# Attention stage: the two norms leave VectorE, a loop is written out, and SyncE's transfers change their order

## The reference, cut to what matters

```python
q = rope(x @ Wq.T); k = rope(x @ Wk.T); v = x @ Wv.T      # 16 maps of 8 dims for each sequence
attn1, attn2 = sdpa(q1, k1, v1), sdpa(q2, k2, v2)          # softmax(q.k * 8**-0.25) @ v
o = attn1 - lam * attn2                                    # 8 heads of 16 values
o = o * rsqrt(mean(o*o over a head) + 1e-8)                # head norm
out = (o * ln_w + ln_b) * (1 - LAMBDA_INIT) @ Wo.T
x = layernorm(x + out)
```

## Time and profile before

| | |
|---|---|
| median of 3 runs | 1077.75 us (1073.69 to 1080.13) |
| the profiled execution, its own time | 1077.57 us |
| its span, first to last instruction | 1075.8 us |
| busy in the span | PE 86%, DVE 86%, POOL 74%, ACT 67% |
| mean granted TensorE clock | 0.957 |
| attention, `scores(0, 0)` to the last residual | 629.0 to 941.6 us |

### The profile page before, as it was taken

One profiled execution on the slowest core, in us unless ns is written; L12 is line 12 of the kernel. 1 busy time (PEld: TensorE's weight loads), 2 busy tenths in 40 slices (PEclk: granted clock), 3 DMA queues, 4 the chain that ended last, 5 costly groups with the idle time before them and its releaser, 6 DMA issues. The chain is left out here.

```text
span 1075.8 us, 15499 instructions
## 1 busy us (share of the span) xinstructions
PE 925.1 (86%) x4482; PEld 481.8 (45%) x4482; DVE 921.2 (86%) x1446; ACT 725.4 (67%) x1536; POOL 791.9 (74%) x576
## 2 busy tenths in 40 slices
PE   7697989797989797777887679999999997799995
PEld 2233434243434342335555454555555543345454
DVE  4799999999999999999883667898999974589996
ACT  4776868686868686444654467777777768777872
POOL 2899999989898989866777644566676534877772
PEclk9899999999999999898998889999999999999997
DMA  4752525253535342005201223232323210000001
GB/s 150 313 237 78 232 83 206 110 198 117 199 117 199 117 198 118 1 1 106 40 1 48 70 75 105 75 99 83 104 74 105 76 46 2 1 1 13 18 20 30
DMA packets 35164, 103.97 MB, mean 97 GB/s; under 512 B 3659, under 2 KB 22475, under 8 KB 24395
## 3 DMA queue, kind: packets, MB, share of 16 engines
q1 hardware_dynamic: 35095, 103.16, 27.9%
HBM read 93.84 MB, written 8.91 MB: 96 GB/s over the span
## 5 line engine op out<-in xcount | busy, mean ns | idle before, releaser
L610 PE MATMUL bank<-m_hC,ident 128*128 128x512 f32 x512 | 256.5, 625 | 61.8 <-POOL m_hC L568 23.5
L558 POOL TENSOR_TENSOR m_dBu<-m_du,m_Bt 128x1024 f32<-128x1024 f32 x128 | 299.5, 2358 | 11.9 <-DMA m_Bt<-bcd 11.1
L333 DVE TENSOR_TENSOR_SCAN bank<-bank,m_dBu 128x512 f32<-128x512 f32 x184 | 222.1, 1218 | 16.4 <-ACT bank L461 12.6
L1406 DVE TENSOR_REDUCE a_nm<-bank 128x2 f32<-128x512 f32 x256 | 169.3, 684 | 45.5 <-PE bank L1637 43.1
L1576 ACT ACTIVATE late<-bank 128x512 f32<-128x512 f32 x256 | 150.4, 598 | 75.3 <-PE bank L1637 73.7
L610 PEld LDWEIGHTS bank<-m_hC,ident 128*128 128x128 f32 x512 | 93.8, 195 | 201.9 <-issue 112.7
L461 ACT ACTIVATE bank<-m_delta,early 128x510 f32<-128x510 f32 x256 | 170.0, 677 | 0.3
L342 DVE TENSOR_TENSOR m_hC<-bank,m_Ct 128x512 f32<-128x512 f32 x184 | 122.7, 667 | 0.0
L568 POOL TENSOR_TENSOR m_hC<-m_hS,m_Ct 128x512 f32<-128x512 f32 x72 | 94.8, 1316 | 25.9 <-DVE m_hS L333 25.8
L1637 PE MATMUL bank<-ks,qs 72*128 72x256 bf16 x512 | 100.1, 279 | 14.5 <-DMA ks<-parts 8.0
L458 ACT ACTIVATE bank<-m_zero 128x2 f32<-128x2 f32 x181 | 31.2, 172 | 113.7 <-DVE m_hC L342 113.3
(11 more groups left out here) (218 smaller groups left out, 1843.6 us busy)
## 6 DMA issues: line engine op xcount, KB each, us to landing
m_Bt<-bcd SPq DMA_DIRECT2D x32, 1024.0 KB, 5.6
m_Ct<-bcd SPq DMA_DIRECT2D x32, 1024.0 KB, 6.4
qs<-parts SPq DMA_DIRECT2D x16, 576.0 KB
ks<-parts SPq DMA_DIRECT2D x48, 192.0 KB
parts<-a_part SPq DMA_DIRECT2D x32, 192.0 KB, 2.2
out<-x_all SPq DMA_DIRECT2D x8, 256.0 KB, 2.3
vx<-in_vrow SPq DMA_DIRECT2D x4, 256.0 KB
qs<-in_fill SPq DMA_DIRECT2D x1, 768.0 KB
```

Source lines behind the costliest of these rows:

```text
L333: nc.vector.tensor_tensor_scan(out, decay, dBu[:, g % RD], 0.0, ALU.mult, ALU.add).then_inc(scan_ready, 1)
L558: nc.gpsimd.tensor_tensor(dBu[:, g % RD:g % RD + CH], du[:, n % 2], Bt[:, s].unsqueeze(1).broadcast_to([P, CH, GTOK]), ALU.mult).then_inc( ...
L610: return nc.tensor.matmul(out, lhsT, rhs, start=start, stop=stop)
L1406: nc.vector.tensor_reduce(nm[:, slot % 2, q, 2 * pair:2 * pair + 2], s1[i % 2][:], AX.X, ALU.max, negate=True).then_inc(max_ready, 1)
```

## The change

The step is rearranged in five ways.

1. **Layer norm.** The output weights are centred once (`wo_c`: the mean of each row is subtracted), so that the projection's result has mean zero over the features; the layer norm then needs only the mean of squares. ACT computes it with two Square instructions that also sum (`squares`), POOL adds the epsilon, takes the power and multiplies once. DVE keeps the addition of the residual.
2. **Head norm.** The product with the reciprocal root goes from DVE (u = 5 of the next step) to POOL (directly behind the power, at u = 14).
3. **Places.** The difference and its followers go to earlier slots; queries and keys of group n + 4 are projected at u = 4 and u = 6 and exchange their banks; POOL's `rotate` waits for the difference; ACT's copy of part 0 goes from u = 0 to u = 15 of the step before; POOL's first subtraction goes ahead of the layer norm.
4. **SyncE.** The transfers of the maxima are issued behind the read back of queries and keys instead of ahead of the wait for the parts.
5. **Loop.** Steps 3 to 10 are written out.

```diff
     def sync(sp):
         def body(n, slot):
@@
             if has(n, 3):
                 sp.wait_ge(split_p, 2 * m + 2)
                 for i in range(2):
                     sp.dma_start(k.parts[i].rearrange("a p t -> p a t"), part[:, :, i, :]).then_inc(parts_out, 16)
-            if has(n, 1):
-                sp.wait_ge(nmT_ready, n + 2)
-                for a in range(3):
-                    sp.dma_start(qs[MROW + a:MROW + a + 1, (slot + 1) % RING],
-                                 nmT[MAPS * a:MAPS * a + MAPS, :]).then_inc(nm_in, 16)
             if has(n, 3):
                 sp.wait_ge(parts_out, 32 * m + 32)
...
                 for a in range(3):
                     sp.dma_start(ks[24 * a:24 * a + 24, s].rearrange("r m t -> r (m t)"), k3).then_inc(q_in, 16)
+            if has(n, 1):
+                sp.wait_ge(nmT_ready, n + 2)
+                for a in range(3):
+                    sp.dma_start(qs[MROW + a:MROW + a + 1, (slot + 1) % RING],
+                                 nmT[MAPS * a:MAPS * a + MAPS, :]).then_inc(nm_in, 16)
@@ vector
-        nc.vector.tensor_scalar(wo_w[:], wo, col("lnwc"), 1.0 - LAM0, ALU.mult, ALU.mult).then_inc(const_ready, 1)
+        nc.vector.tensor_reduce(wo_mean[:], wo, AX.X, ALU.add).then_inc(const_ready, 1)
+        nc.vector.tensor_scalar(wo_mean[:], wo_mean[:], -1.0 / DM, None, ALU.mult).then_inc(const_ready, 1)
+        nc.vector.tensor_scalar(wo_c[:], wo, wo_mean[:, 0:1], None, ALU.add).then_inc(const_ready, 1)
+        nc.vector.tensor_scalar(wo_w[:], wo_c[:], col("lnwc"), 1.0 - LAM0, ALU.mult, ALU.mult).then_inc(const_ready, 1)
...
-        def head_norm(m):
-            dve.wait_ge(rms_chain, 2 * m + 2)
-            wait(dve, o_turned, m)
-            nc.vector.tensor_tensor(on[:].rearrange("p q (h v) -> p (q h) v", v=VW), o[:],
-                                    rms[:].unsqueeze(2).broadcast_to([P, TS * NH, VW]), ALU.mult).then_inc(on_ready, 1)
...
-            dve.wait_ge(r_ready, m + 1)
-            layer_norm_stats(dve, nc, r, stats, mv, veps, stat_chain, 3 * m)
-            nc.vector.tensor_scalar(veps[:], mv[:, :, 1], LN_EPS, None, ALU.add).then_inc(stat_chain, 1)
...
-                if u == 5 and has(n, -2):
-                    head_norm(n - 2)
-                if u == 8 and has(n, -1):
+                if u == 6 and has(n, -1):
                     leave(n - 1, 1)
-                if u == 9 and has(n, -1):
+                if u == 7 and has(n, -1):
                     difference(n - 1)
-                if u == 13 and has(n, -1):
+                if u == 11 and has(n, -1):
                     mean_square(n - 1)
-                if u == 15 and has(n, -2):
+                if u == 14 and has(n, -2):
                     residual(n - 2)
@@ gpsimd
         def rotate(m):
             pool.wait_ge(qk_ready, 2 * m + 2)
+            wait(pool, o_ready, min_group(m - 4, BATCH))
...
+        def head_norm(m):
+            pool.wait_ge(ms_ready, m + 1)
+            nc.gpsimd.tensor_tensor(ms_eps[:], ms[:], eps[:], ALU.add).then_inc(rms_chain, 1)
+            nc.gpsimd.tensor_tensor(rms[:], ms_eps[:], k.neg_half[:, 0:TS * NH], ALU.pow).then_inc(rms_chain, 1)
+            nc.gpsimd.tensor_tensor(on[:].rearrange("p q (h v) -> p (q h) v", v=VW), o[:],
+                                    rms[:].unsqueeze(2).broadcast_to([P, TS * NH, VW]), ALU.mult).then_inc(on_ready, 1)
...
         def normalize(m):
-            pool.wait_ge(stat_chain, 3 * m + 3)
+            pool.wait_ge(var_ready, m + 1)
+            nc.gpsimd.tensor_tensor(veps[:], var[:], ln_eps[:], ALU.add).then_inc(norm_step, 1)
             nc.gpsimd.tensor_tensor(rstd[:], veps[:], k.neg_half[:, 0:TS], ALU.pow).then_inc(norm_step, 1)
-            nc.gpsimd.tensor_tensor(nmean[:], mv[:, :, 0], neg_one[:], ALU.mult).then_inc(norm_step, 1)
-            nc.gpsimd.tensor_tensor(shift[:], nmean[:], rstd[:], ALU.mult).then_inc(norm_step, 1)
-            nc.gpsimd.tensor_tensor(scaled[:], r[:], rstd[:].unsqueeze(2).broadcast_to([P, TS, P]),
-                                    ALU.mult).then_inc(norm_step, 1)
-            nc.gpsimd.tensor_tensor(k.x_all[:, bass.ds(TS * m, TS), :], scaled[:],
-                                    shift[:].unsqueeze(2).broadcast_to([P, TS, P]), ALU.add).then_inc(norm_chain, 1)
+            nc.gpsimd.tensor_tensor(k.x_all[:, bass.ds(TS * m, TS), :], r[:],
+                                    rstd[:].unsqueeze(2).broadcast_to([P, TS, P]), ALU.mult).then_inc(norm_chain, 1)
...
+                if u == 0 and has(n, 3):
+                    residual_high(n + 3)
                 if u == 0 and has(n, -3):
                     normalize(n - 3)
-                if u == 2 and has(n, 3):
-                    residual_high(n + 3)
@@ scalar
+        def squares(m):
+            act.wait_ge(r_ready, m + 1)
+            wait(act, norm_chain, m)
+            for t in range(TS):
+                last = nc.scalar.activation(square[:, t], r[:, t], ACT.Square, scale=DM ** -0.5,
+                                            accum_out=var[:, t:t + 1])
+            last.then_inc(var_ready, 1)
...
-                if u == 0 and has(n, 3):
-                    m = n + 3
...
+                if u == 15 and has(n, -2):
+                    squares(n - 2)
+                if u == 15 and has(n, 4):
+                    m = n + 4
                     act.wait_ge(rope, 2 * m + 2)
                     wait(act, parts_out, 32 * m)
                     wait(act, split_p, 2 * m)
                     nc.scalar.activation(part[:, 0], rot[:], ACT.Copy).then_inc(split_a, 1)
...
-                if u in ((7, 9) if lone(n) else (5, 6)) and has(n, 4):
+                if u in ((7, 9) if lone(n) else (5, 7)) and has(n, 4):
@@ tensor
-                if u in ((6, 8) if lone(n) else (4, 5)) and has(n, 4):
+                if u in ((6, 8) if lone(n) else (4, 6)) and has(n, 4):
...
-                if u == 6 and has(n, -1):
+                if u == 5 and has(n, -1):
                     turn_sums(n - 1, 1)
...
-                if u == 8 and has(n, -2):
+                if u == 9 and has(n, -2):
                     pe.wait_ge(on_ready, n - 1)
...
-                if u == 14 and has(n, 0):
+                if u == 15 and has(n, 0):
                     turn_sums(n, 0)
@@ parts
-            with eng.Fori(0, 2) as i:
-                for d in range(ATT_RING):
-                    alone(attention(ATT_RING * i + d + 3, (d + 3) % ATT_RING))
-            for n in range(11, 15):
+            for n in range(3, 15):
                 alone(attention(n, n % ATT_RING))
```

More of the change, by code:

```diff
@@ L1283, in attention_phase @@
     r = late("r", [P, TS, P])
-    stats = sb("stats", [P, TS, 6])
-    mv = sb("mv", [P, TS, 2])
+    wo_c = sb("wo_c", [P, DM])
+    wo_mean = sb("wo_mean", [P, 1])
+    var = sb("var", [P, TS])
+    ln_eps = sb("ln_eps", [P, TS])
     veps = sb("veps", [P, TS])
     rstd = sb("rstd", [P, TS])
[L1288 to L1291, removed]
+    square = late("square", [P, TS, P])
     ma, mb = k.bank[0:2]
@@ L1334, in attention_phase @@
     r_ready = sem("r_ready")
-    stat_chain = sem("stat_chain")
-    rstd_ready = sem("rstd_ready")
+    var_ready = sem("var_ready")
     norm_step = sem("norm_step")
@@ L1387, in vector @@
         nc.vector.tensor_reduce(lam2[:], lam4[:], AX.X, ALU.add).then_inc(lam_chain, 1)
-        nc.vector.tensor_scalar(wo_w[:], wo, col("lnwc"), 1.0 - LAM0, ALU.mult, ALU.mult).then_inc(const_ready, 1)
-        dve.wait_ge(const_ready, 2)
+        nc.vector.tensor_reduce(wo_mean[:], wo, AX.X, ALU.add).then_inc(const_ready, 1)
+        dve.wait_ge(const_ready, 3)
+        nc.vector.tensor_scalar(wo_mean[:], wo_mean[:], -1.0 / DM, None, ALU.mult).then_inc(const_ready, 1)
+        dve.wait_ge(const_ready, 4)
+        nc.vector.tensor_scalar(wo_c[:], wo, wo_mean[:, 0:1], None, ALU.add).then_inc(const_ready, 1)
+        dve.wait_ge(const_ready, 5)
+        nc.vector.tensor_scalar(wo_w[:], wo_c[:], col("lnwc"), 1.0 - LAM0, ALU.mult, ALU.mult).then_inc(const_ready, 1)
         nc.vector.tensor_scalar(lnb[:], lnb[:], col("lnbc"), None, ALU.mult).then_inc(const_ready, 1)
-        dve.wait_ge(const_ready, 4)
+        dve.wait_ge(const_ready, 7)
         def negative_lambda():
@@ L1440, in difference @@
                 dve.wait_ge(lam_chain, 5)
-            wait(dve, osq_ready, m)
+            wait(dve, on_ready, m)
             pairs = av[:].rearrange("p q g e v -> p (q g) e v")
@@ L1494, in gpsimd @@
         nc.gpsimd.memset(eps[:], 1e-8).then_inc(eps_ready, 1)
-        nc.gpsimd.memset(neg_one[:], -1.0).then_inc(eps_ready, 1)
+        nc.gpsimd.memset(ln_eps[:], LN_EPS).then_inc(eps_ready, 1)
         pool.wait_ge(eps_ready, 2)
@@ L1552, in body @@
                 if u == 14 and has(n, -1):
[L1553 to L1558, removed]
+                    head_norm(n - 1)
                 yield
@@ L1613, in body @@
                     nc.scalar.activation(nmT[:], ma[:].bitcast(BF16)[0:3 * MAPS, 0:SEQ], ACT.Copy).then_inc(nmT_ready, 1)
```

(26 more changed lines are left out.)

14 lines of the change are left out of this document (9 added, 5 removed).

## The result

| | before | after |
|---|---|---|
| median | 1078.94 us (4 runs, 1073.69 to 1080.34) | 1152.43 us (4 runs, 1150.79 to 1154.92) |
| profiled execution, its span | 1077.57, 1075.8 us | 1153.15, 1151.4 us |
| mean granted TensorE clock | 0.957 | 0.927 |

The ratio is 1.0696 with the 95% interval [1.0664, 1.0727]: 7% slower. The prediction had the direction, and its range ended at 1140: the size was too small.

What follows compares the result with a forecast made beforehand. The prediction took the ring of the maxima to bound the changed kernel: steps of 9.4 + 12.2 = 21.6 us. Start + 3.8, thirteen steps + 42.8 and end - 2.5 added 44.1 to 1077.6, giving 1122 us, range 1094 to 1140.

Steps and rivals of the forecast that it cites:

- the ring of the maxima: Attention step: from u = 0 to L1360, plus L1360 to the maxima's landing, sets the step at 21.6 us; likeliest, 0.55.
- 3 to 5 us each: Sign: PE's longest waits in steps 0 to 13, before `scores(n, 0)`, ended by the maxima's DMA, of this length.
- 5 us or more: Sign: the transfers of the maxima land this long after issue instead of 1.8 us.
- L1360 to L1360 20 to 22: Sign: distance in us between the parts' write outs of successive attention steps.
- the last steps are a little shorter: Sign: the attention steps from n = 13 on, without query and key transfers, gain from VectorE's relief.
- The price of the clock: First half of the attention step: half speed for 4 us after PE's wait, 8.1 us becoming 9.4.
- The landing: Second half of the attention step: maxima wait for the read back and land 12.2 us after the parts' write out.
- The start: Ahead of the thirteen steps: `scores(0, 0)` comes at 632.8 instead of 629.00, + 3.8 us.
- The end: Five last steps, without query and key transfers: VectorE's relief gives 0 to 6 us, taken as - 2.5 us.
- VectorE's 2.5 us a step: Attention step: VectorE loses norm work and a slow difference, its busy time falling to some 13.5 of 17.6 us.
- (a): Rival, attention steps: maxima queue but the clock doesn't fall; steps of 20.3 us, 1105 us in all; chance 0.26.
- (b): Rival, attention steps: maxima pass the reads, landing at + 8.8; steps some 17.2 us, 1061 us in all; chance 0.12.

Runs made afterwards that it cites:

- e2: The kernel before with only SyncE's new order (maxima issued behind the read back of queries and keys): 1155.80 us, ratio 1.0722.
- e1: The changed kernel with SyncE's old order alone (maxima ahead of the wait for the parts): 1071.80 us, ratio 0.9956.
- e3: The changed kernel with 22 extra matmuls of 512 columns on PE ahead of its wait for the maxima: 1131.31 us, ratio 1.0492.
- e8: The kernel before with the loop over steps 3 to 10 written out and nothing else: 1073.86 us, ratio 0.9988.
- e10: The changed kernel with the maxima issued between queries and keys, and the copies of parts 1 and 2 two slots earlier: 1050.90 us, ratio 0.9754.
- e4: The changed kernel with the maxima issued between the queries' transfer and the three of the keys: 1072.96 us, ratio 0.9959.
- e7: The changed kernel with the maxima issued by ScalarE at u = 9 instead of by SyncE: 1072.38 us, ratio 0.9978.
- e9: The changed kernel with the maxima issued by ScalarE and the copies of parts 1 and 2 two slots earlier: 1082.86 us, ratio 1.0042.

## Why the direction was right, and which terms of the sum failed

The mechanism is shown. The maxima wait behind the read back, PE's longest waits stand before `scores(n, 0)` and are ended by them, and the ring of the maxima sets the step; e2 makes it alone, e1 unmakes it. Of the tests named, "3 to 5 us each" came out at 3.9 to 6.5, and "5 us or more" at 5.5 at the median. "L1360 to L1360 20 to 22" failed (24.1), and so did "the last steps are a little shorter" for the stretch as a whole.

What failed are two terms of the step, forecast at 9.4 + 12.2 = 21.6 us. At the mean of the thirteen steps of the trace they are 10.6 + 13.3 = 23.8, and they are the whole miss per step:

1. **The price of the clock.** I let half speed last "4 us, some less than the 5.4 us seen after 635.65", and took off 0.7 us for backlogs that would vanish: 8.1 at full clock became 9.4, + 1.3. No row carried "some less". Measured, half speed lasts 6.3 us in the step shown. e3 has the same first half without the fall, 8.3 us at the mean, so the fall costs 2.3 (10.6 - 8.3), 1.0 more than forecast, and the rest is 0.2 above the 8.1. Of the 11.18 us in the step shown, `scores(n, 4)` starts at 7.47, where 4.86 + 2.0 was assumed; exp 4 follows 1.32 us after it (852.62 - 851.30), so what was taken for ScalarE's backlog did not go. It is program order: two copies stand between exp 3 and exp 4, and from the start of one exponential to that of the other it is 1.23 us before (799.98 - 798.75) and after (852.62 - 851.39). L1358 comes 2.39 us after exp 4 (before: 2.55).
2. **The landing.** Forecast 2.76 + 8.96 + 0.3 + 0.2 = 12.2 us behind L1358, measured 13.3 at the mean, 1.1 more. L1365 starts 2.9 us after L1358 (2.75 in the step shown, but 3.7 and 3.9 in two others). By the semaphore events the read back lands 9.65 us after L1365, against 8.96 + 0.2; in the kernel before the mean is already 9.3, so the 8.96, from a single step, was short. That is the largest part of the miss, 0.5. The maxima land 0.6 us behind it, not 0.3. The 0.3 came from `scl` behind `kb`, one small transfer behind one large; here 24 rows of the maxima stand behind the last large packets.

Together these are 2.2 us a step (23.8 - 21.6), times 13 is + 29, against + 71.7 - 42.8 = + 28.9.

**The start** was + 3.8, measured + 2.0. This is in part luck: the landing is 1 us longer than assumed, but L1358 of step -1 starts at 617.87, 2.7 us earlier than in the kernel before. In e2, with the same order of SyncE, it starts at 623.37 and `scores(0, 0)` comes at 636.6.

**The end** was - 2.5, measured + 1.8, and the relief is in it. Steps 14 and 15, up to their last scores, take 14.5 and 12.5 us instead of 15.6 and 13.9, together - 2.5; the other runs with the moved norms have 14.5 to 14.7 and 12.5 (e3, with its extra matmuls, aside), and e2, without them, has 15.6 and 13.9. Two things cover it. Step 13, behind a wait of 5.98 us and at a clock of 0.86, takes 17.9 instead of 16.1 us, + 1.8. And from the last scores to the end of the span it is 165.6 us instead of 163.2, + 2.5; in the other runs with the moved norms it is 163.8 to 166.0, in e2 and e8 163.0 and 163.1, so at least part of this comes with the moved norms or their places. Why was not looked into.

**Costed at nothing, and right:** ScalarE's squares stand inside PE's wait (863.62 in the step shown, with PE idle until 868.11); the loop (e8, whose regular step is 17.55 us against 17.57), so neither register work nor new code shows; GpSimd's wait in `rotate`. **VectorE's 2.5 us a step** came as forecast (16.0 to 13.4) and was worth nothing beside the ring. With the old order nothing can be seen of it in a step either: 17.66 in e1, but 17.66 in e8 too, which has no relief, and 17.87 in the kernel before. Only with the ring gone (e10, 16.61) does a step come below what the earlier trace rows had as PE's busy time.

**The rivals.** (a), queued with the clock up, is e3: the ring without the fall, 21.4 us at the mean of thirteen and not 20.3, for the landing (13.2 instead of 12.2) and a first half of 8.3. (b), maxima passing the reads, occurred for half of their rows only, and PE waits for all of them. Its threshold, a landing before L1360 + 9.7, was sound: e4 lands them at + 9.7 at the mean and is level with before or better. The Trainium skill's rule weighed in the prediction ("DMA: Bandwidth & Descriptors", section "Queues, rings and completion order") agrees with the landings of 5.5 us and with the 24 rows that moved last; e7 and e9 show that leaving the queue is not enough, which that rule alone does not tell.

## What to carry to other kernels

Give the transfers of one queue the order in which their data are needed, and for each way round write down the ring: from the step's start to the issue, plus the issue to the landing behind all that is in flight, whichever queue issues it. Before relieving an engine, look for such a ring of the same length as the step; here 2.5 us off VectorE changed no step that could be measured while a ring was the bound. And a wait on PE costs more than its own length where the clock falls in it: take the duration of the half clock from the longest row seen, not a shorter one (even the 5.4 us seen were fewer than the 6.3 that came). Judge a landing by the last transfer that is waited for, not by the median of all.

## What the runs showed of the hardware that was not expected

- A transfer of 8 KB lands in 1.8 us alone, in 4.2 us behind 576 KB in its queue, in 5.5 us behind 1152 KB, and in 5.2 us at the median when another engine issues it while those reads are in flight (e9). For three of them, from the first issue to the last landing, it is 3.1, 5.7, 7.2 and 7.9 us.
- Behind 1152 KB half of the 48 rows moved at once, and the other half only with the last large packets, in 13 of 14 steps of the kernel after.
- After a wait of some 4.5 us TensorE stayed at half clock for 6.3 us, though it was busy from the restart on; 22 more matmuls a step made the step 2.6 us shorter (e3).
- The same VectorE instruction takes 0.48 us in all 16 groups in a slot where GpSimd is held back, against 1.40 us at the median beside `rotate`.
- Three small transfers issued by ScalarE cost it some 1.8 us a step (24.6 us over 14 steps, e7), as much as they cost SyncE (1.82 us), but there exponentials stand behind them.
